# Two bodies for TensorE's loop over blocks of nodes: one with the branches for further edge tiles, one without, chosen once per turn of eight blocks

## The reference

```python
for _ in range(DEPTH):                      # DEPTH = 3
    msgs = jnp.take(h, src, axis=0)
    msgs = jax.nn.relu(msgs @ W_edge + b_edge)
    agg = jax.ops.segment_sum(msgs, dst, num_segments=N_NODES)
    h = jax.nn.relu(jnp.concatenate([agg, h], axis=-1) @ W_agg + b_agg)
```

## Time and profile before

| | us |
|---|---|
| median of the runs | 4142.66 (4136.66, 4142.66, 4155.34) |
| the profiled execution, own time | 4142.93 |
| its span | 4141.2 |
| PE busy in the span | 3617.9 |
| DVE busy in the span | 3215.0 |
| POOL busy in the span | 2885.6 |

### The profile page before, as it was taken

One profiled execution on the slowest core, in us unless ns is written; L12 is line 12 of the kernel. 1 busy time (PEld: TensorE's weight loads), 2 busy tenths in 40 slices (PEclk: granted clock), 3 DMA queues, 4 the chain that ended last, 5 costly groups with the idle time before them and its releaser, 6 DMA issues. The chain is left out here.

```text
span 4141.2 us, 98637 instructions
## 1 busy us (share of the span) xinstructions
PE 3617.9 (87%) x19764; PEld 2407.4 (58%) x19765; DVE 3215.0 (78%) x11124; ACT 2268.0 (55%) x4904; POOL 2885.6 (70%) x2867
## 2 busy tenths in 40 slices
PE   5777759999989999799996888888888589999997
PEld 3555548888778888677774444444444244444443
DVE  7888866777767777688884688888888579999998
ACT  1333325555545555466664445445444267777777
POOL 3777757777477776677772777777777377777775
PEclk8999979999999999999998899999999799999999
DMA  2555548888778887688885455555555234444443
GB/s 83 178 175 172 176 134 242 252 252 252 220 220 255 252 251 238 209 263 275 268 261 163 140 159 155 155 161 153 155 161 155 81 104 130 131 127 128 131 131 90
DMA packets 583565, 749.57 MB, mean 181 GB/s; under 512 B 146958, under 2 KB 407786, under 8 KB 583398
## 3 DMA queue, kind: packets, MB, share of 16 engines
q1 hardware_dynamic: 476774, 554.65, 41.1%
q0 software_dynamic: 106624, 193.25, 18.1%
HBM read 426.01 MB, written 321.54 MB: 181 GB/s over the span
## 5 line engine op out<-in xcount | busy, mean ns | idle before, releaser
L797 POOL DMA_INDIRECT mp_gathered<-msg_rows,other_idx x784 | 753.2, 961 | 306.5 <-issue 190.5
L559 POOL DMA_INDIRECT by_window<-so_pay,so_pos_i x392 | 387.3, 988 | 165.9 <-issue 114.6
L1090 POOL DMA_INDIRECT ll_gathered<-msg_rows,other_idx x392 | 372.6, 950 | 168.1 <-issue 104.2
L815 PE MATMUL bank<-mp_edge_hot,mp_gathered 128*128 128x256 bf16 x3528 | 458.4, 274 | 20.3 <-POOLq L785 15.6
L1676 POOL DMA_INDIRECT ff_agg<-at_rows,last_idx x392 | 383.1, 977 | 115.9 <-issue 107.2
L1376 POOL DMA_INDIRECT at_of_src<-x_rows,kv_idx x392 | 375.3, 958 | 119.3 <-issue 118.4
L1380 POOL DMA_INDIRECT at_of_dst<-x_rows,node_idx x392 | 371.5, 948 | 119.4 <-issue 119.4
L870 ACT ACTIVATE mp_h_out<-bank,mp_b_agg 128x256 f32<-128x256 f32 x392 | 185.9, 474 | 422.7 <-PE bank L832 417.2
L903 DVE TENSOR_SCALAR mp_edge_hot<-digits,mp_first_col,column 128x256 bf16<-128x256 bf16 x1176 | 342.1, 361 | 65.3 <-issue 52.0
L815 PEld LDWEIGHTS bank<-mp_edge_hot,mp_gathered 128*128 x3528 | 346.8, 98 | 68.2 <-issue 22.6
L1788 PE MATMUL bank<-ff_h_cols,ff_w 128*128 128x512 f32 x784 | 371.7, 597 | 0.9 <-ACT ff_h_cols L1821 0.9
(11 more groups left out here) (252 smaller groups left out, 8937.3 us busy)
## 6 DMA issues: line engine op xcount, KB each, us to landing
msg_rows<-mp_msg_out SPq DMA_DIRECT2D x392, 192.0 KB
mp_h_in<-h_cols SPq DMA_DIRECT2D x392, 128.0 KB
h_cols<-mp_h_out SPq DMA_DIRECT2D x392, 128.0 KB
msg_rows<-so_msg_out SPq DMA_DIRECT2D x98, 384.0 KB
h_cols<-so_h_out SPq DMA_DIRECT2D x98, 256.0 KB
ll_h_in<-h_cols SPq DMA_DIRECT2D x196, 128.0 KB
x_rows<-ll_x SPq DMA_DIRECT2D x98, 256.0 KB
skip_rows<-ll_skip SPq DMA_DIRECT2D x98, 256.0 KB
```

The lines of the kernel that those rows point to most:

```text
L559: pool.indirect_dma_start(core.by_window, bass.IndirectOffsetOnAxis(ap=pos_i[k][:, t:t + 1], axis=0), pay[k][:, t, :], None, bounds_check= ...
L797: pool.indirect_dma_start(gathered[:, r * PARTS * D:(r + 1) * PARTS * D], None, core.msg_rows[layer % 2], bass.IndirectOffsetOnAxis(ap=cor ...
L815: product = nc.tensor.matmul(agg_bank[k], gathered[:, bass.ds(at + d * D, D)], hot, start=(first and d == 0), stop=True, skip_group_check= ...
L1090: pool.indirect_dma_start(gathered[:, r * PARTS * D:(r + 1) * PARTS * D], None, core.msg_rows[(LAYERS - 1) % 2], bass.IndirectOffsetOnAxis ...
```

## The change

Each first word of a turn gets a flag, bit 18, if any of the turn's eight blocks has a further tile. The sort stage computes the flags with one more reduction and two small operations. PE's loop body now stands twice inside the loop: behind the load of the words, a branch on the flag (L743) leads to a body with the Ifs or to one (L745) without them. DVE keeps its one body with the Ifs. The words' upper half is now masked (`& 511`) wherever it is read, on PE and on DVE, since the flag sits above it. The blocks written out straight keep their Ifs.

```diff
-                nc.vector.tensor_copy(core.spans[0:1, 0:NW], word_f[:, :]).then_inc(base_ok, 1)
...
+                nc.vector.tensor_reduce(turn_more[:, :], more_f[:, 0:FLAGGED].rearrange("a (t k) -> a t k", k=MSGS), AXX, ALU.max).then_inc(base_ok, 1)
...
+                nc.vector.tensor_scalar(turn_more[:, :], turn_more[:, :], 0.0, float(FLAG), ALU.is_gt, ALU.mult).then_inc(base_ok, 1)
...
+                nc.vector.tensor_tensor(word_f[:, 0:FLAGGED:MSGS], word_f[:, 0:FLAGGED:MSGS], turn_more[:, :], ALU.add).then_inc(base_ok, 1)
...
+                nc.vector.tensor_copy(core.spans[0:1, 0:NW], word_f[:, :]).then_inc(base_ok, 1)
...
+        def plain_or_further(eng, turn):
...
+            with aligned(eng, 1, FLAGGED // MSGS) as j:
+                def looped(further_too):
+                    for r in range(MSGS):
+                        turn(lambda lag, step: step(MSGS * j + r + lag, (r + lag) % MSGS, j + (r + lag) // MSGS), further_too, True)
+                load_words(eng, MSGS * j)
+                with eng.If((words[eng.engine][0] >> 18) > 0):
+                    looped(True)
+                with eng.Else():
+                    looped(False)
...
-            return word & 511, word >> 9
+            return word & 511, (word >> 9) & 511
...
-                        further(pe, n, first, final, more)
+                        if further_too:
+                            further(pe, n, first, final, more)
...
-                    blocks(pe, turn, MSGS)
+                    plain_or_further(pe, turn)
```

More of the change, by code:

```diff
@@ L38 @@
 HOTS = 4
+FLAG, FLAGGED = 1 << 18, NW // MSGS * MSGS
 LAST = (N - (NG - 1) * GR) // T
@@ L44 @@
 assert NW % RING == 0 and NT % CHUNK == 0 and TILES % CHUNK == 0 and ALWAYS + BEHIND * CHUNK < TILES - 2 * CHUNK
-assert NG % 2 == 0 and (N - (NG - 1) * GR) % T == 0 and N == E
+assert FLAG > 511 * 512 + 511 and NG % 2 == 0 and (N - (NG - 1) * GR) % T == 0 and N == E
 def reached(eng, sem, count, base=0):
@@ L220, in sort_by_window @@
         first_f, word_f, more_f, all_f = (sb("so_" + n, [1, NW]) for n in ("first_f", "word_f", "more_f", "all_f"))
+        turn_more = sb("so_turn_more", [1, FLAGGED // MSGS])
         counts, incl, base_row = sb("so_count", [1, LOW]), sb("so_incl", [1, LOW]), sb("so_base", [1, LOW])
@@ L360, in _ @@
                 nc.vector.memset(core.spans[0:1, NW:NW + RING], 0)
-                nc.vector.tensor_copy(core.spans[0:1, 0:NW], word_f[:, :]).then_inc(base_ok, 1)
                 nc.vector.tensor_scalar(more_f[:, :], more_f[:, :], 0.0, None, ALU.max).then_inc(base_ok, 1)
+                dve.wait_ge(base_ok, 10)
+                nc.vector.tensor_reduce(turn_more[:, :], more_f[:, 0:FLAGGED].rearrange("a (t k) -> a t k", k=MSGS), AXX, ALU.max).then_inc(base_ok, 1)
+                nc.vector.tensor_tensor_scan(all_f[:, :], more_f[:, :], more_f[:, :], 0.0, ALU.add, ALU.bypass).then_inc(base_ok, 1)
                 dve.wait_ge(base_ok, 11)
-                nc.vector.tensor_tensor_scan(all_f[:, :], more_f[:, :], more_f[:, :], 0.0, ALU.add, ALU.bypass).then_inc(base_ok, 1)
+                nc.vector.tensor_scalar(turn_more[:, :], turn_more[:, :], 0.0, float(FLAG), ALU.is_gt, ALU.mult).then_inc(base_ok, 1)
                 dve.wait_ge(base_ok, 12)
@@ L367, in _ @@
                 dve.wait_ge(base_ok, 13)
+                nc.vector.tensor_tensor(word_f[:, 0:FLAGGED:MSGS], word_f[:, 0:FLAGGED:MSGS], turn_more[:, :], ALU.add).then_inc(base_ok, 1)
+                dve.wait_ge(base_ok, 14)
                 nc.vector.tensor_copy(core.more_before[:, :], all_f[:, :]).then_inc(base_ok, 1)
+                dve.wait_ge(base_ok, 15)
+                nc.vector.tensor_copy(core.spans[0:1, 0:NW], word_f[:, :]).then_inc(base_ok, 1)
             @block.tensor
@@ L713, in message_passing, with load_words, straight, do @@
         words = {}
[L715 to L720, removed]
+        def load_words(eng, n):
+            words[eng.engine] = nc.values_load_multi_w_load_instructions(
+                core.spans[0:1, bass.ds(n, MSGS)], engines=[eng.engine], min_val=0, max_val=2 * FLAG - 1,
+                skip_runtime_bounds_check_because="the flag is compared, both halves are masked and only address tables of their size")[1]
+        def plain_or_further(eng, turn):
+            def straight(n):
+                def do(lag, step):
+                    if 0 <= n + lag < NW:
+                        step(n + lag, (n + lag) % MSGS, (n + lag) // MSGS)
+                turn(do, True, False)
+            for n in range(MSGS):
+                straight(n)
+            with aligned(eng, 1, FLAGGED // MSGS) as j:
[7 more added lines that the diff above has]
+                    looped(False)
+            for n in range(FLAGGED, NW + 5):
+                straight(n)
+        def edge_tiles(eng, n, r, ahead=False):
+            if r == 0 and not ahead:
+                load_words(eng, n)
             word = words[eng.engine][r]
-            return word & 511, word >> 9
+            return word & 511, (word >> 9) & 511
         def further(eng, n, first, last, more):
@@ L817, in add_tile, with sum_edges @@
                         return product
-                    def sum_edges(n, r, j):
+                    def sum_edges(n, r, j, further_too, ahead):
                         def more(i, at):
@@ L823, in more @@
                             add_tile(r % 2, i + 1, more_hot[:, bass.ds((at & 1) * W, W)]).then_inc(tile_mm[layer], 1)
-                        first, final = edge_tiles(pe, n, r)
+                        first, final = edge_tiles(pe, n, r, ahead)
                         pe.wait_ge(edge_hot_ok, wins + n + 1)
@@ L852, in count_targets, with turn @@
                         counted.then_inc(dst_mm, 1)
-                    def turn(do):
-                        do(0, sum_edges)
+                    def turn(do, further_too, ahead):
+                        do(0, lambda n, r, j: sum_edges(n, r, j, further_too, ahead))
                         do(0, count_targets)
@@ L1015, in last_layer, with load_words, plain_or_further, straight @@
         words = {}
[L1017 to L1022, removed]
+        def load_words(eng, n):
+            words[eng.engine] = nc.values_load_multi_w_load_instructions(
+                core.spans[0:1, bass.ds(n, TURN)], engines=[eng.engine], min_val=0, max_val=2 * FLAG - 1,
+                skip_runtime_bounds_check_because="the flag is compared, both halves are masked and only address tables of their size")[1]
+        def plain_or_further(eng, turn):
+            def straight(n):
+                def do(lag, step):
+                    if 0 <= n + lag < NW:
+                        step(n + lag, (n + lag) % TURN, (n + lag) // TURN)
+                turn(do, True, False)
+            for n in range(2 * TURN):
+                straight(n)
+            with aligned(eng, 2, FLAGGED // TURN) as j:
+                def looped(further_too):
+                    for r in range(TURN):
+                        turn(lambda lag, step: step(TURN * j + r + lag, (r + lag) % TURN, j + (r + lag) // TURN), further_too, True)
+                load_words(eng, TURN * j)
+                with eng.If((words[eng.engine][0] >> 18) > 0):
+                    looped(True)
+                with eng.Else():
+                    looped(False)
+            for n in range(FLAGGED, NW + 2 * TURN):
+                straight(n)
+        def edge_tiles(eng, n, r, ahead=False):
+            if r == 0 and not ahead:
+                load_words(eng, n)
             word = words[eng.engine][r]
-            return word & 511, word >> 9
+            return word & 511, (word >> 9) & 511
         def further(eng, n, first, last, more):
@@ L1154, in turn @@
                 do(-10, group(skip_product))
-            blocks(pe, turn)
+            plain_or_further(pe, turn)
         @block.scalar
```

## The result

The changed kernel takes 4168.25 us (median of 6 runs, 4165.27 to 4176.43), the kernel before 4147.68 us (6 runs, 4136.66 to 4155.34). The ratio is 1.0058 with a 95% interval from 1.0047 to 1.0069: slower, by some 24 us by the ratio (20.6 us between the two medians). The forecast was 4170.

The account below looks back on a forecast made before the run. PE bounds the first two layers, DVE paces the last. Terms 10.9 + 1.8 + 7.8 + 2.8 + 0.6 + 3 = 26.9 us on 4142.9 gave 4170 us; 8-in-10 range 4144 to 4192, forecast's chance 0.58.

Parts of the forecast that it names:

- plain turns, first two layers: PE's 30 unflagged turns: seven Ifs hidden under the sequencer's lead over the matmuls, block 0's If swapped for the test; 0.
- flagged turns, first two layers: PE's sequencer pays test, mask and far jump where its lead is used up: 0.68 x 16 = 10.9, plus masks 1.8 us.
- masks on DVE, last layer: One more register operation per DVE If delays the queued product by 0.08 us, 98 times: +7.8 us.
- flagged turns, last layer, without masks: The same 0.68 us on PE in 7 turns, partly covered by DVE: 0.4 a turn, +2.8 us.
- code met for the first time: Fetch at first entry of the second body in three loops: 0 to 7.8 us, taken as +3.
- table: Three more small operations in DVE's chain in the sort stage, for the flags: +0.6 us.
- rival (b): Plain turns gain 13.2 us (4157); or DVE's masks and last-layer flagged turns hide too (4146, no measurable change); chance 0.27.
- estimate of 0.36 us: Cost of a flagged turn by the skill's branch times instead of 0.68; the sum would be 4165 us.
- rival (a): Last layer paced by PE's issue, not DVE; masks hide and L1125's 26.3 us wait could go: 4136 us; chance 0.08.
- Rival (c): Two bodies do not stay in instruction memory together; each change of body costs 2.0 us, 66 in all: 4236; chance 0.07.

Follow-up runs that it names:

- experiment 2: Changed kernel, but DVE reads a second word table without flags, so it needs no mask: 4165.75 us, ratio 1.0059 to the kernel before.
- experiment 4: Kernel before plus a never-true If in each of the last four blocks of a turn, PE's loops, first two layers: 4155.31 us, ratio 1.0029.
- experiment 8: Changed kernel with an unflagged table for DVE and PE's words, flag included, loaded ahead in two halves: 4150.55 us, ratio 1.0020 to the kernel before.
- experiment 1: Changed kernel with the flag set in every turn, so the body without Ifs never runs: 4195.9 us, ratio 1.0124 to the kernel before.
- experiment 3: Kernel before plus one never-true If in each turn's first block, PE's loops, first two layers: 4159.83 us, ratio 1.0036.
- experiment 6: Kernel before with PE's eight words loaded ahead in two halves during previous work, one body, no flag: 4122.87 us, ratio 0.9952.
- experiment 7: Kernel of experiment 6 with DVE's words also loaded ahead in the last layer: 4115.55 us, ratio 0.9930 to the kernel before.

## Why the prediction came out right, step by step

| term of the sum, us | forecast | measured |
|---|---|---|
| plain turns, first two layers | 0 | -3.5 (28 turns, as the table of the result counts them) |
| flagged turns, first two layers | +12.7 | +11.4 (14 x 0.71, and 0.71 for each of the two first ones) |
| masks on DVE, last layer | +7.8 | +6 to +6.6 |
| flagged turns, last layer, without masks | +2.8 | +1.0 (turns 3 to 23 of experiment 2 against before; +2.7 on DVE's own timeline) |
| code met for the first time | +3 | +16 |
| table | +0.6 | not seen |

*Plain turns.* The step held: a flag test came in, an If went out, and they cancel (2.72 and 1.23 us against 2.53 and 1.40). That the other seven Ifs were hidden is shown by experiments 4 and 8. The 0.13 us that each plain turn won in the table is a matter of counting: with the step into a turn counted to that turn, they grew by 0.02 us. So the first half of rival (b) falls: the two steps around a plain turn's start lost 0.53 us against twice the steady 2.51 before, and lose 0.55 now.

*Flagged turns.* The mechanism held: experiments 1 and 3 show that it is sequencer work at the place where the lead is used up. The size was put too high, and that 0.71 lies so near to 0.68 is in part luck. The forecast was 0.68 us a turn, 0.79 with the masks at further tiles. The 0.71 include the step into the next turn; with each step counted to the turn that it leads into, 0.48 are left, and the jump at the turn's end is then counted to the next. Experiment 1, where every turn pays for test, mask and jump and the way of counting matters little, gives 0.53 for what was priced at 0.68, and plain and flagged turns together cost 7.9 us, not 12.7. One part was priced too high: the far jump takes 0.17 us once it has been run, not the 0.287 of the loop's entry. One of the 14 turns (turn 14 of the first layer, +1.72 us) also met the lower clock, 0.50 from 913.2 to 916.6 us; the other 13 grew by 0.64.

The prediction also gave an estimate of 0.36 us by the branch times of the Trainium skill, "Advanced Engine Details and Errata", section Control Flow Timing (about 108 ns for a compare-and-branch, 51 ns for a branch-always). It had left out the gaps that the 0.68 holds; with them the estimate would be some 0.47 us, nearer to the measured 0.53 than the 0.68 is. Branch by branch the trace differs from these figures: on PE's sequencer the test took 77 to 87 ns falling through and 208 to 223 ns taken, and the far jump 169 to 173 ns.

*Masks on DVE.* The term held: 22 turns by 0.30 us are 6.6, the gap ahead of most products grew by 0.07 us where 0.08 was forecast, and experiment 2 gave 6.0 us back in turns 3 to 23. So rival (b)'s second half falls too. In the last layer DVE is the pacer, as forecast: experiment 6 shortens PE's turn start and moves nothing there, experiment 7 shortens DVE's and each turn gets 0.65 us shorter. So rival (a) falls. My reading of the gaps had left out the largest gap of the turn, the load.

*Code met for the first time.* This is the term that was mis-sized: the step "0 if it is already there, 3 x 2.6 = 7.8 if not; I take 3". It took the loop's entry for the dearest case, though the earlier trace rows puts its 2.60 us down to DVE's hot matrices, so they were no measure of a fetch. A first jump over a whole body took 4.4, 4.3 and 5.7 us. Behind it PE's clock was low for a stretch, which cost the next block of the first two layers another 1.3 us. Together this is 10.3 us in the first two layers (turns 1 and 2, less what a flagged turn costs anyway) and 5.6 in the last. Rival (c), that the bodies do not stay together, falls: later branches took 0.22 us at most, and no instruction packet came to queue q8 from 672 to 1120 and from 1220 to 1655 us. In the last layer's loop the last one came at 1770.5 us, when the flagged body was first entered. The rule of the Trainium skill ("Runtime: NRT & Kernel Launch", Instruction fetch mechanics), by which a taken branch to a target outside a window of two pages forces a fetch, agrees with each first jump (q8 had 3, 3 and 5 packets around them) and not with the later ones.

The measured terms add up to some 31 us, as do the three layers. The whole execution shows 24 us by the ratio and 23.5 by the spans, since the untouched rest was 7.2 us shorter. So the forecast of 26.9 owes its fit to luck in good part, to errors of opposite sign: 13 us missed in one term, 8 to 9 us too much in the others, and that scatter.

## What to carry to other kernels

Before a branch is moved out of a loop, look at how far the sequencer runs ahead there: where the lead stands at its ceiling the branch is free, and only what stands at the place where the lead is used up (here a load of registers and the branch to a further tile) is worth moving. Here the register load was worth 20 us on PE and another 9 to 13 on DVE, the branches nothing. A second copy of a loop body has a price of its own, 2.7 to 6.0 us for the first jump over it and, where TensorE idles meanwhile, a block at the lower clock behind it. This counts when a loop is short (23 turns).

## What was not expected of the hardware

The same jump instruction took 4.38 us the first time and 0.17 us in every later flagged turn, though the loop now holds two bodies. Behind the 4.90 us for which PE idled there, the granted clock was 0.60 for 4.3 us. A wait of 0.78 us that the profile gave to PE belonged to a register load of 0.6 us on the waiting engine's own sequencer. One more register operation of 45 ns ahead of a branch on DVE moved the products behind it by 0.07 us, although those start 0.35 us or more behind the start of the last hot matrix.
